# Gated cross-attention and expert kernel: order and queues of the first loads, statistics of x by pairs, and 16 weight pieces ahead of the first item

## What is computed

```
x += tanh(g_xattn[0]) * attention0(layernorm(x), ctx, mask)      # 8 heads of 8; each batch: 256 queries by 256 keys
x += tanh(g_ffn[0])   * experts0(layernorm(x))                   # 8 experts 256 -> 512 -> 256, top-p router (0.9)
x += tanh(g_xattn[1]) * attention1(layernorm(x), ctx, mask1)     # one head, keys = values = ctx
x += tanh(g_ffn[1])   * experts1(layernorm(x))                   # 4 experts by position, 256 -> 256 -> 256
```

## Times and profile before

| | us |
|---|---|
| median of 3 runs | 1007.66 |
| lowest and highest run | 1003.5, 1012.44 |
| the profiled execution | 1013.97 |
| its span, from the first to the last instruction | 1012.2 |
| PE busy in the span | 815.8 |
| DVE busy | 779.4 |
| ACT busy | 580.8 |
| POOL busy | 566.8 |

### The profile page before, as it was taken

How to read it: one execution, slowest core, us unless ns; L and a number is a source line. 1 busy time by engine, 2 the same in 40 slices (tenths; PEclk the granted TensorE clock), 3 DMA queues, 4 the chain that set the end, 5 groups by cost and what they waited for, 6 DMA issues and landing times.

```text
span 1012.2 us, 24981 instructions
## 1 busy us (share of the span) xinstructions
PE 815.8 (81%) x9015; PEld 700.1 (69%) x9015; DVE 779.4 (77%) x2496; ACT 580.8 (57%) x1258; POOL 566.8 (56%) x565
## 2 busy tenths in 40 slices
PE   2445656889999999989999899999999688865564
PEld 2334444778888887878878788887788577754553
DVE  4385778898988989889898889989895686655652
ACT  2265777767777776676767577776673132222222
POOL 3253646777787776868777687877563122221110
PEclk9555676999999999999999999999999799987787
DMA  3759999786777887687877867678760400000100
GB/s 126 212 115 222 228 222 198 150 143 127 142 138 140 154 155 142 128 131 147 144 150 145 142 120 147 145 134 144 121 111 12 131 26 12 22 22 22 43 12 21
DMA packets 319520, 122.67 MB, mean 121 GB/s; under 512 B 274716, under 2 KB 312612, under 8 KB 319396
## 3 DMA queue, kind: packets, MB, share of 16 engines
q1 hardware_dynamic: 318656, 120.53, 59.6%
q10 hardware_dynamic: 740, 0.54, 0.2%
HBM read 45.53 MB, written 8.39 MB: 53 GB/s over the span
## 4 chain that ended last, share of the span: by engine, by line
PE 45%; DVE 20%; DMA 12%; issue 10%; ACT 5%; POOL 4%; SPq 3%; POOLq 0%; DVEq 0%; ACTq 0%
PE psU L754 11%; PE psG L754 10%; PE psY L754 8%; DMA p_turn<-p_parts 7%; PE psV L754 4%; PE ps L754 4%; DVE ps L1098 3%; PE psT L754 2%; DVE th_ga_h L1193 2%; PE psM L754 2%; POOL p_parts L530 2%; DMA stage<-in_L_ffn_up_w 2%; DMA stage<-in_L_ffn_gate_w 2%; PE psV L911 2%; DVE psT L1098 1%
## 5 line engine op out<-in xcount | busy, mean ns | idle before, releaser
L530 POOL TENSOR_TENSOR p_parts<-p,p_parts 128x512 f16<-128x512 f32 x256 | 297.6, 1165 | 169.3 <-ACT p_parts L636 155.6
L522 POOL TENSOR_TENSOR hp_lo<-th_ga_h,hp_hi 128x512 f16<-128x512 f32 x128 | 149.3, 1166 | 121.5 <-ACT hp_hi L660 119.0
L754 PE MATMUL psU<-xT,w_gu 128*128 128x256 f16 x1536 | 190.2, 274 | 30.7 <-DVE th_ga_h L1193 29.7
L754 PE MATMUL psG<-xT,w_gu 128*128 128x256 f16 x1536 | 194.4, 278 | 1.3 <-DVE th_ga_h L1185 1.3
L754 PE MATMUL psY<-w_dn,hp_hi 128*128 128x256 f16 x1024 | 183.8, 275 | 1.1 <-POOL hp_lo L522 1.1
L754 PEld LDWEIGHTS psU<-xT,w_gu 128*128 128x128 f16 x1536 | 142.4, 98 | 53.6 <-DVE th_ga_h L1193 37.5
L636 ACT ACTIVATE p_parts<-p 128x512 f16<-128x512 f32 x256 | 161.3, 630 | 27.6 <-DMA p_turn<-p_parts 26.3
L754 PEld LDWEIGHTS psG<-xT,w_gu 128*128 128x128 f16 x1536 | 146.3, 99 | 21.0 <-DVE th_ga_h L1185 1.4
L628 ACT ACTIVATE p<-psT,exp_bias 128x256 f32<-128x256 f32 x256 | 107.8, 475 | 71.2 <-DVE exp_bias L1102 55.7
L754 PE MATMUL psY<-w_dn,hp_lo 128*128 128x256 f16 x512 | 140.4, 274 | 0.0
L628 ACT ACTIVATE p<-ps,exp_bias 128x256 f32<-128x256 f32 x256 | 107.7, 475 | 57.0 <-DVE exp_bias L1102 55.2
(11 more groups left out here) (164 smaller groups left out, 1171.9 us busy)
## 6 DMA issues: line engine op xcount, KB each, us to landing
mask_in<-in_mask_Bx2048x_ff SPq DMA_DIRECT2D x32, 256.0 KB, 3.1
part_scratch<-parts SPq DMA_DIRECT2D x16, 384.0 KB, 3.2
q_stack<-part_scratch SPq DMA_DIRECT2D x62, 96.0 KB
k_stack<-part_scratch SPq DMA_DIRECT2D x62, 96.0 KB
stage<-in_L_ffn_gate_w SPq DMA_DIRECT2D x8, 512.0 KB, 5.0
stage<-in_L_ffn_up_w SPq DMA_DIRECT2D x8, 512.0 KB, 4.8
stage<-in_L_ffn_down_w SPq DMA_DIRECT2D x8, 512.0 KB, 4.5
p_turn<-p_parts SPq DMA_TRANSPOSE x256, 3.5
```

The lines of the kernel that those rows point to most:

```text
L522: pool.tensor_tensor(hp_lo[:, u % 2, :], hb32[:, u % 2, :], hp_hi[:, u % 2, :], ALU.subtract).then_inc(s["h_split"], 1)
L530: pool.tensor_tensor(p_parts[:, g % 4, 1, :, :], p32[:, g % 2, :, :], p_parts[:, g % 4, 0, :, :], ALU.subtract).then_inc(s["plo_done"], 1)
L754: return pe.matmul(out_, lhsT, rhs, start=start, stop=stop, skip_group_check=shares_bank)
```

## The change

- SP's preamble: the first two pairs of x come first; the three weight loads stand between the small loads, in another order; the second mask comes after the stacks of pair 0; instead of 14 pairs of x only two follow.
- The other pairs of x come two at a time, from SP at place 4 of the steps 2, 6, 10 and so on. DVE takes their statistics at place 3 of the steps 0, 4, 8, ..., 24, POOL their power at place 5. Before, DVE took those of all 14 in the places 0 to 6 of step 0.
- The weight loads 3 to 23 are issued by ACT, each behind the second `w_high` of the load three before it, and no longer by SP.
- `W_AHEAD` is 16. The first two pieces are done between the first projection of q and k and that of v.
- The memsets of `k_stack` and `v_parts`, by POOL before, and the second half of `q_stack` are done by DVE at its program's start.

The diff, cut to its core (the list of semaphore names left out):

```diff
--- before.py
+++ after.py
@@ -54,7 +54,7 @@
 W_PIECES = 6 * NE
-W_AHEAD = 8
+W_AHEAD = 16
 TAIL_STEP = B + 1
...
@@ -284,8 +284,7 @@
             if q < 2:
-                eng.wait_ge(s["stacks_set"], 2)
-                eng.wait_ge(s["q_zeroed"], q + 1)
+                eng.wait_ge(s["stacks_set"], 3)
             hh, i = piece // 2, piece % 2
@@ -306,6 +305,19 @@
+        def load_weight_stage(eng, c):
+
+            e, m = c // 3, c % 3
+            if e:
+                eng.wait_ge(s["wgrp_T"], 2 * (c - 3) + 2)
+            if m < 2:
+                src = A[("L0_ffn_gate_w", "L0_ffn_up_w")[m]][e].rearrange("(t p) h -> p t h", p=P)
+                dst = stage[m].rearrange("p (t h) -> p t h", t=IB)
+            else:
+                src = A["L0_ffn_down_w"][e].rearrange("(t p) i -> p t i", p=P)
+                dst = stage[m].rearrange("p (t i) -> p t i", t=2)
+            eng.dma_start(dst, src).then_inc(s[f"stage{m}_loaded"], 16)
+
         steps = range(LATE_START + ROUNDS + 1)
@@ -315,18 +327,8 @@
-            def load_weight_stage(c):
-
-                e, m = c // 3, c % 3
-                if e:
-                    sp.wait_ge(s["wgrp_T"], 2 * (c - 3) + 2)
-                if m < 2:
-                    src = A[("L0_ffn_gate_w", "L0_ffn_up_w")[m]][e].rearrange("(t p) h -> p t h", p=P)
-                    dst = stage[m].rearrange("p (t h) -> p t h", t=IB)
-                else:
-                    src = A["L0_ffn_down_w"][e].rearrange("(t p) i -> p t i", p=P)
-                    dst = stage[m].rearrange("p (t i) -> p t i", t=2)
-                sp.dma_start(dst, src).then_inc(s[f"stage{m}_loaded"], 16)
+            def load_x(r):
+                sp.dma_start(x_res[:, r:r + 2, :], x_d[:, r:r + 2, :]).then_inc(s["x_loaded"], 16)
@@ -400,8 +402,8 @@
                         load_stacks(sp, 1 - par, q + 1, i + 2)
-                    if i % 2 == 0 and 6 + g // 2 < 3 * NE:
-                        load_weight_stage(6 + g // 2)
+                    if (n % 4, i) == (2, 4) and n + 6 <= NPAIR * 2 - 2:
+                        load_x(n // 2 + 3)
                 if n == TAIL_STEP:
@@ -417,23 +419,22 @@
+            sp.dma_start(x_res[:, 0:2, :], x_d[:, 0:2, :]).then_inc(s["x01_loaded"], 16)
             load_small_weight(0, "wst_loaded")
             load_small_weight(1, "wst_loaded")
-            sp.dma_start(x_res[:, 0:2, :], x_d[:, 0:2, :]).then_inc(s["x01_loaded"], 16)
             sp.dma_start(ctx_in[:, 0, :], ctx_d[0]).then_inc(s["ctx0_loaded"], 16)
+            load_weight_stage(sp, 0)
             load_small_weight(2, "wv_loaded")
+            load_weight_stage(sp, 1)
+            sp.dma_start(ctx_in[:, 1, :], ctx_d[1]).then_inc(s["ctx1_loaded"], 16)
             load_mask(0, 0)
-            for c in range(3):
-                load_weight_stage(c)
-            sp.dma_start(ctx_in[:, 1, :], ctx_d[1]).then_inc(s["ctx1_loaded"], 16)
-            load_mask(1, 1)
+            load_weight_stage(sp, 2)
             store_parts(0, 0)
                 load_stacks(sp, 0, 0, piece)
-            sp.dma_start(x_res[:, 2:16, :], x_d[:, 2:16, :]).then_inc(s["x_loaded"], 16)
+            load_mask(1, 1)
+            load_x(2)
             store_parts(1, 1)
-            for c in range(3, 6):
-                load_weight_stage(c)
             sp.wait_ge(s["v_projected"], 1)
@@ -487,9 +488,7 @@
-            pool.memset(k_stack[:, :, :, :, :], 1.0).then_inc(s["stacks_set"], 1)
-            pool.memset(v_parts[:, :, :, :, :], 1.0).then_inc(s["stacks_set"], 1)
-            pool.wait_ge(s["stacks_set"], 2)
+            pool.wait_ge(s["stacks_set"], 3)
             for piece in range(4):
@@ -508,13 +507,13 @@
-            def pow1():
-                pool.wait_ge(s["ln_in"], 1)
-                pool.tensor_tensor(rstd[:, 2:16], rstd[:, 2:16], minus_half[:, 2:16], ALU.pow).then_inc(s["pow_done"], 1)
+            def pow1(r):
+                pool.wait_ge(s["ln1_in"], r // 2)
+                pool.tensor_tensor(rstd[:, r:r + 2], rstd[:, r:r + 2], minus_half[:, 0:2], ALU.pow).then_inc(s["pow1_done"], 1)
-                pool.wait_ge(s["ln_in"], 2 + pair)
+                pool.wait_ge(s["ln_in"], 1 + pair)
                 pool.tensor_tensor(rstd2[:, :], ve2[:, :], minus_half[:, 0:1], ALU.pow).then_inc(s["pow_done"], 1)
@@ -532,7 +531,7 @@
-                pool.wait_ge(s["ln_in"], 1 + NPAIR + 2 * j + i + 1)
+                pool.wait_ge(s["ln_in"], NPAIR + 2 * j + i + 1)
                 pool.tensor_tensor(crs[:, :], cve[:, :], minus_half[:, 0:2], ALU.pow).then_inc(s["pow_done"], 1)
@@ -544,8 +543,8 @@
                     g, hp, half = 8 * n + i, i // 2, i % 2
-                    if (n, i) == (0, 6):
-                        pow1()
+                    if (n % 4, i) == (0, 5) and q + 2 < NPAIR:
+                        pow1(q + 2)
                     if 1 <= g <= 8 * B:
@@ -610,6 +609,8 @@
                                ).then_inc(s["w_hi"], 1)
+                if k == 1 and 3 * e + m + 3 < 3 * NE:
+                    load_weight_stage(act, 3 * e + m + 3)
@@ -662,14 +663,16 @@
             copy_qk(0)
+            for w in range(2):
+                w_high(w // 6, w % 6 // 2, w % 2)
             copy_qk(1)
+            for w in range(2, 4):
+                w_high(w // 6, w % 6 // 2, w % 2)
             act.wait_ge(s["gate_loaded"], 32)
             act.activation(gates[:, :], gate_in[:, :], ACT.Tanh).then_inc(s["gates_ready"], 1)
-            for w in range(W_AHEAD // 2):
-                w_high(w // 6, w % 6 // 2, w % 2)
             for piece in range(2, 4):
                 load_stacks(act, 0, 0, piece)
-            for w in range(W_AHEAD // 2, W_AHEAD):
+            for w in range(4, W_AHEAD):
                 w_high(w // 6, w % 6 // 2, w % 2)
@@ -893,11 +896,13 @@
             project_qk(0, 0)
+            for w in range(2):
+                weight_transposes(w // 6, w % 6 // 2, w % 2)
             pe.wait_ge(s["qk_copied"], 2)
             project_qk(1, 1)
-            for w in range(W_AHEAD):
+            for w in range(2, W_AHEAD):
                 weight_transposes(w // 6, w % 6 // 2, w % 2)
@@ -1052,7 +1057,9 @@
             dve.sem_inc(s["w_split"], 2)
-            dve.memset(q_stack[:, 0, :, :, :, :], 0.0).then_inc(s["q_zeroed"], 1)
+            dve.memset(q_stack[:, :, :, :, :, :], 0.0).then_inc(s["stacks_set"], 1)
+            dve.memset(k_stack[:, :, :, :, :], 1.0).then_inc(s["stacks_set"], 1)
+            dve.memset(v_parts[:, :, :, :, :], 1.0).then_inc(s["stacks_set"], 1)
             st.link(dve.memset(low_max[:, :, :], LOG_P_SCALE))
@@ -1074,8 +1081,8 @@
                     dve.wait_ge(s["pow01_done"], 1)
-                if q == 2:
-                    dve.wait_ge(s["pow_done"], 1)
+                elif q % 2 == 0:
+                    dve.wait_ge(s["pow1_done"], q // 2)
                 dve.tensor_scalar(xn[:, :], x_res[:, q, :], mean_var[:, q, 0:1], rstd[:, q:q + 1],
@@ -1135,7 +1142,7 @@
             def norm2(pair):
-                dve.wait_ge(s["pow_done"], pair + 2)
+                dve.wait_ge(s["pow_done"], pair + 1)
                 dve.wait_ge(s["qk_projected"], min(pair + 3, NPAIR))
@@ -1214,7 +1221,6 @@
             norm1(1)
-            dve.memset(q_stack[:, 1, :, :, :, :], 0.0).then_inc(s["q_zeroed"], 1)
             for w in range(W_AHEAD):
@@ -1246,7 +1252,7 @@
             def late_norm(j, i):
-                dve.wait_ge(s["pow_done"], 1 + NPAIR + 2 * j + i + 1)
+                dve.wait_ge(s["pow_done"], NPAIR + 2 * j + i + 1)
                 if i:
@@ -1347,12 +1353,10 @@
                         add_expert(done, half)
-                    if (n, i) == (0, 0):
-                        dve.wait_ge(s["x_loaded"], 16)
-                    if n == 0 and i < 7:
-                        norm1_stats(2 + 2 * i, 4 + 2 * i)
-                    if (n, i) == (0, 6):
-                        norm1_var(2, NPAIR, s["ln_in"])
+                    if (n % 4, i) == (0, 3) and q + 2 < NPAIR:
+                        dve.wait_ge(s["x_loaded"], 16 * (q // 2 + 1))
+                        norm1_stats(q + 2, q + 4)
+                        norm1_var(q + 2, q + 4, s["ln1_in"])
                     if (n % 2, i) == (0, 4) and q + 1 < NPAIR:
                     if tail is not None and (n % 2, i) == (0, 6):
```

More of the change, by code:

```diff
@@ L126, in build @@
         bd = sb("bd", [P, P], F32)
-        names = """x01_loaded ln01_in pow01_done stacks_set q_zeroed bias_set bias_turned biasT_ready x_loaded
+        names = """x01_loaded ln01_in pow01_done stacks_set bias_set bias_turned biasT_ready x_loaded
             wst_loaded wv_loaded brow_loaded bias_v_loaded gate_loaded rt_loaded stage0_loaded stage1_loaded stage2_loaded ctx0_loaded ctx1_loaded
@@ L131, in build @@
             v_copied x1_done lg_done y_used x3_done d_upT wst_T router_T wgrp_T
-            w_split bias_ready ln_in pow_done xn_ready qk_projected v_projected qk_copied w_hi
```

(1 more changed line is left out.)

## The result

The changed kernel takes **1001.25 us** (median of 20 runs, 995.66 to 1009.99) against 1010.67 us of the kernel before, measured beside it (20 runs, 1003.5 to 1015.1). The ratio of the mean times is 0.9918, 95% interval 0.9892 to 0.9944: 8.3 us faster, just under 1%; the medians lie 9.4 us apart. The profiled executions are 1002.5 us (span 1000.7) and 1013.97 us (span 1012.2). They lie 11.5 us apart, so the profiles flatter the change by 2 to 3 us.

The account below looks back on a forecast made before the run. It took waits for late weight loads and step 0's statistics to hold the first 40 items, then the DMA engines; PE and DVE are busy later. +1 - 21 + 7 = -13 from 1013.97 gives 1001, as median 995 us; range 984 to 1010.

Parts of the forecast that it names:

- rival B: 40 items: DMA engines hold them at share 1.0, so 103 us; gain only 6 us, 1002 us; chance 0.25.
- Start: Before item 0: eight more pieces ahead, item 0 at about 45.5 instead of 45.0 us; +1 us, bounds -1 and +6.
- longer price: DVE's memsets at the start: ones written element by element, `k_stack` 3.5 and `v_parts` 1.4 us, instead of 1.76 and 0.7.
- The pair of pieces at 2.6 us: Before item 0: two pieces, one per bank, need 2.6 us for transposes, ACT, DVE and gaps; seven pairs 18.2 us.
- Items: Items 0 to 40, steps 0 to 4: weight waits and statistics vanish, DMA engines come next; 98 us, -21 us.
- I take 80: Steps 0 to 3: remaining DMA work of 84.6 us fits into 80 us at a share of 1.06.
- share times length: 40 items: DMA work as busy share times stretch length, 107.8 us, falling to 101.6 with four loads fewer.
- sign that I had named for a failure: Items staying at 115 us with waits for `stage` merely replaced by waits for `p_turn` would prove the prediction wrong.
- Later steps: Steps 8, 12, 16, 20, 24: DVE's late statistics and five x loads cost +7 us, bounds +1 and +10.
- 1.2 us each comes through: Steps 8 to 24, place 4: statistics of 1.5 us less 0.3 of DVE's slack delay each step; 6 us in all.
- Rival C: Later steps: DVE's 1.2 us delay is taken up before PE needs it, 989 us; chance 0.13.
- Rival D: ACT's load issues stall, 2.8 us each, holding the exponentials; +25, 1033 us; chance 0.12.

Follow-up runs that it names:

- after_again2: The changed kernel itself, unaltered, measured and profiled once more: 1000.46 us, ratio 0.9882 to the kernel before.
- e6: Changed kernel without the statistics and powers of x pairs 6 to 15 (steps 8, 12, 16, 20, 24): 997.52 us, ratio 0.9856.
- ahead_24: Changed kernel with 24 pieces ahead of the first item in place of 16: 1005.67 us, ratio 0.9944.
- e5: Changed kernel with the memsets of `k_stack` and `v_parts` back on POOL: 1003.52 us, a single run.
- e3: Changed kernel with loads 10 to 23 issued by SP at every second place, ACT issuing only 3 to 9: 1004.24 us, ratio 0.9927.
- e7: Changed kernel with 8 pieces ahead and loads 6 to 23 issued by SP, ACT issuing only 3 to 5: 997.08 us, ratio 0.9858.
- e2: Changed kernel with 8 pieces ahead of the first item in place of 16: 996.43 us, ratio 0.9837.
- e8: e7 with the memsets of `k_stack` and `v_parts` on POOL and a pair's statistics taken singly at places 1 and 2: 992.51 us, ratio 0.9796.
- e4: Changed kernel with loads 11 to 23 cut to half their bytes, number of transfers unchanged: 996.58 us, ratio 0.9848.
- e9: e8 with the loads left to ACT as in the change: 994.62 us, ratio 0.9837.
- e1: Kernel before with only x changed: pairs, statistics at place 3, power at place 5; queues, memsets and `W_AHEAD` stay: 1001.12 us, ratio 0.9886.

## Why the prediction was right, and where its terms were off

The median, 1001.25 us, is inside the range of 984 to 1010, and the gain of 8.3 us is of the forecast's sign. It stayed under the 1% that I had given a chance of 0.58 to be passed. Of the 6 us between 995 and 1001, 3 are the base: the kernel before has a median of 1010.67 over 20 runs, not 1007.66. That base also moves the measured median onto rival B's 1002 us; as a gain, 8 to 9 us lie between B's 6 and the forecast's 13.

The sum came closer than its terms, and that is luck. In the profiled executions they are -1.8, -11.1 and +1.4 us, together -11.5, against +1, -21 and +7, together -13: the items fell short by 10 us, and the two others made up for 8. With the second execution of the change they are -0.3, -15.4 and -2.7.

**Start.** Forecast +1, measured -1.8, and -0.3 and +0.6 in the two other executions of the same start (after_again2, e6). The first is outside the bound of -1, the mean of the three, -0.5, is not. The parts, in the first: the DVE memsets cost their longer price (3.47 and 1.39 us, forecast 3.5 and 1.4); they end at 11.23 instead of 9.9, with 0.80 and 0.28 us of gaps and a later begin; Wv's product starts at 11.80 (forecast 12.2), the projection at 14.31 (13.7). The remaining 14 pieces begin at 21.64 (22.8) and item 0's scores at 43.18 (45.5). The pair of pieces at 2.6 us is right: in ahead_24 pairs follow each other every 2.59 us. What I had too dear was what stands between them, 4.4 us of ACT's stack issues; all in all there are 21.5 - 18.2 = 3.3 us, and some of these are two waits for loads (1.55 and 1.04 us), so the loads didn't quite keep up. The step that failed in substance is the reason: I let the memsets on DVE remove `xn`'s stretching, and e5 shows that the earlier x alone removes it.

The Trainium skill ("VectorE: DVE Perf Modes", zero memsets issued as uint32) has a memset take one cycle per element whatever the type, and so spoke for the longer price: 4096 ones in bf16 take 3.47 us, as long as 4096 words of zeros, so the trace agrees. The section treats zeros alone; that ones can't be issued as words was my reading of it.

**Items.** Forecast -21, measured -11.1; in the second execution, 103.6 us, -15.4. The term that was mis-sized is "I take 80": steps 0 to 3 took 91.0 and 86.7 us, while step 4 took 16.9 against 18. I read the shares of 1.06 to 1.12 as what the DMA engines could keep up, and they are values of stretches, not of the whole: over all 40 items the mean is 1.00 after, with 0.92 in step 0 and 0.94 in step 3. The second fault is that I priced the remaining work by share times length. That product should have fallen from 107.8 to 101.6 with four loads fewer, and it came out at 107.9 and 103.6. With the same loads it is 99 with SP issuing (e3), and for 17 loads 109 with SP (e7) and 125 with ACT (e2). So it isn't a fixed amount of work that can be divided by a better share. The rate in GB/s is steadier: in all kernels with full loads and 8 or 16 pieces ahead it was 195 (e5) to 217 (e8), whatever queue issued them.

The waits of 20.9 us did vanish, as predicted, and were replaced by waits for `p_turn`. That is one half of the sign that I had named for a failure; the other, items at 115 us, didn't come.

Of rival B this much is shown: the bytes of the loads lengthen the items (e4), and the issuer changes which wait is seen more than the length (e3, and e8 with e9). That the DMA engines are full throughout isn't shown. Step 0 takes 16.9 us with its loads, bytes halved gave back only 4 to 8 of 11.5 us, and ahead_24 and the chain in step 3 say that the turning of the pieces on PE, ACT and DVE is part of what a load costs there. No kernel here has the pieces without the bytes, so how the rest divides between that work and the transposes' time in flight stays open.

The Trainium skill ("DMA: Bandwidth & Descriptors", "Issuing engines are not separate DMA queues") had said that a second issuer saves only its sequencer's time. The trace agrees within its scatter: 106.0 us of items with SP's loads, 103.6 and 107.9 with ACT's; 111.3 and 111.6 in e8 and e9.

**Later steps.** Forecast +7, measured +1.4 and -2.7 in the two profiled executions of the change, against one of the kernel before. That difference is within the scatter and says little of the term; e6 says more. "1.2 us each comes through" was nearly right: 1.0 us in each of the five steps, though by other terms (2.4 of DVE's time, 0.9 back from `on`), and 1.5 to 5 us over the stretch. The place was wrong: PE's waits for `th_ga_h`, which I expected to double at place 4, stayed at 13.9 us in all, longest 0.8 (before 14.0 and 0.9), and it waits 0.8 us for `o_rec` instead. Rival C, the statistics hidden, isn't borne out by the steps' lengths; how much of the 5 us arrives at the end isn't settled by the medians.

**Rival D** is refuted: ACT's load issues take 0.37 to 0.47 us.

**What I had not asked.** No rival said that 16 pieces ahead might be worse than 8. The two terms were in my sum, each in a sum of its own: pieces ahead cost 2.6 us a pair, and a load less in the items was given 1.8. Put side by side they speak against the step. Measured over kernels of like kind:

| pieces ahead | item 0 at | items | item 40 at | ratio to before |
|---|---|---|---|---|
| 8 (e7, e2) | 37.0, 38.0 | 110.3, 117.0 | 147.2, 154.9 | 0.9858, 0.9837 |
| 16 (change twice, e3) | 45.9 to 47.5 | 103.6 to 107.9 | 151.0 to 153.8 | 0.9882 to 0.9927 |
| 24 | 58.8 | 99.3 | 158.2 | 0.9944 |
| 8, with memsets and statistics moved (e8, e9) | 34.7, 35.7 | 111.3, 111.6 | 145.9, 147.3 | 0.9796, 0.9837 |

In the means of the first three rows eight pieces (four loads) move item 0 from 37.5 to 46.4 and to 58.8 us, which is 2.2 and 3.1 us a load, and shorten the items from 113.6 to 105.8 and to 99.3, 1.9 and 1.6 us a load. From 16 to 24 that is a loss of 6 us at item 40. From 8 to 16 it is only about 1 us there, less than the scatter, although the ratios are 2 to 9 us apart; that 8 is better is shown by the times, and why isn't shown whole. The gain of the change is there with x alone (e1), and 16 pieces ahead give a part of what the rest could bring back.

## What to carry to other kernels

Before moving a transfer to another queue, ask whether it is late because of its issuer or because the DMA engines are full: halve its bytes in a trial, and if the time follows, expect a new queue mostly to move the wait to another tile. Work pulled ahead of a pipeline must be priced against what the pipeline would have hidden of it: here a pair of weight pieces with its load costs 2.2 to 3.1 us before the first item and 1.6 to 1.9 us inside. Don't divide a sum of DMA busy time by a better share: the sum moved with the issuer. When two edits aim at one stall (an earlier load and a moved memset at the first norm), try each alone, since one may do it all and the other only cost.

## What the runs showed of the hardware

- Loads make DMA transposes in flight slower, on a second queue somewhat more than in the transposes' own. Median from issue to landing over the 40 items: 17 loads by ACT 5.2 and 5.3 us (e2, e9), by SP 4.6 and 4.6 (e7, e8); 13 loads by ACT 4.7 and 4.4 (the change), by SP 4.3 (e3), with half their bytes 3.9 (e4). In step 4 of the change, without loads, it is 3.6 and 3.8.
- The busy share of the DMA engines isn't a measure of work left to do. Share times length over the items is 109 us with SP's loads and 125 with ACT's for the same transfers (e7, e2), 110 against 115 (e8, e9), 99 against 108 and 104 (e3, the change).
- Time on DVE and POOL beside each other is not additive. `rstd<-mean_var` over 128x2 takes 0.17 us alone and 1.14 beside POOL, `on` over 128x128 0.29 or 1.20, `xn` over 128x256 0.41 or 4.37 to 4.86 beside memsets of 3.5 and 1.4 us. A shift of 2 us of one engine moves the loss from one instruction to another, so inserted work can cost less, or more, than its own duration.
- These memsets cost nearly the same on either engine: 128x4096 ones in bf16 3.47 us on DVE and 3.51 on POOL, 128x1600 1.39 and 1.43.
